# Norm, router and combining weights of a batch moved inside the attention of the next batch

## The reference

```python
mod = (_silu(L0_c) @ L0_wmod).reshape(L0_c.shape[0], 6, 1, -1)
h = _layernorm(x) * (1 + ca) + sa
x = x + ga * attention(h)             # scores * scale + relative-position bias, softmax, values, o_w
h = _layernorm(x) * (1 + cb) + sb
probs = sigmoid(h @ router_w.T + expert_bias)
top_w, top_idx = top_k(probs, 8);  top_w = 2.5 * top_w / (sum(top_w) + 1e-9)
h1w = silu(einsum('th,eih->eti', h, w_gate)) * combine.T[:, :, None]   # combine: top_w at top_idx, else 0
x = x + gb * (einsum('eti,ehi->th', h1w, w_down) + silu(h @ w_gate_shared.T) @ w_down_shared.T)
```

## Time and profile before

| | |
|---|---|
| median of 3 runs | 1000.38 us (1000.25 to 1002.1) |
| the profiled execution | 999.45 us, of which the span of instructions is 997.2 us |
| busy in the span | PE 946.7 us (95%), DVE 767.4 (77%), ACT 678.3 (68%), POOL 398.2 (40%) |
| chain that ended last, by engine | PE 84%, DMA 5%, DVE 4%, ACT 2%, POOL 2% |
| attention ends (last `attend`) | about 500 us from the span's start |
| mean granted clock of PE | 0.988 of full speed |

### The profile page before, as it was taken

One profiled execution on the slowest core, in us unless ns is written; L12 is line 12 of the kernel. 1 busy time (PEld: TensorE's weight loads), 2 busy tenths in 40 slices (PEclk: granted clock), 3 DMA queues, 4 the chain that ended last, 5 costly groups with the idle time before them and its releaser, 6 DMA issues.

```text
span 997.2 us, 15699 instructions
## 1 busy us (share of the span) xinstructions
PE 946.7 (95%) x4592; PEld 685.8 (69%) x4592; DVE 767.4 (77%) x1452; ACT 678.3 (68%) x1168; POOL 398.2 (40%) x260
## 2 busy tenths in 40 slices
PE   4889999999999999999979699999999999999997
PEld 2546666666666666666524578888888888888886
DVE  5757667766676666767546689999999999999997
ACT  4656666666666666666536577777777777777775
POOL 0668888888888888888800000000000000000000
PEclk9999999999999999999979899999999999999999
DMA  7985445445553564355002999999999999999991
GB/s 210 274 224 125 97 118 127 117 95 128 128 120 81 117 149 110 82 128 127 22 0 75 213 218 221 220 220 223 222 221 225 221 222 223 222 222 222 222 208 43
DMA packets 71105, 160.57 MB, mean 161 GB/s; under 512 B 10272, under 2 KB 36192, under 8 KB 60944
## 3 DMA queue, kind: packets, MB, share of 16 engines
q1 hardware_dynamic: 71056, 159.97, 71.2%
HBM read 105.60 MB, written 2.42 MB: 108 GB/s over the span
## 4 chain that ended last, share of the span: by engine, by line
PE 84%; DMA 5%; DVE 4%; ACT 2%; POOL 2%; SPq 1%; issue 1%; POOLq 0%; ACTq 0%; DVEq 0%
PE ps L620 40%; PE ps L433 11%; PE ps L420 10%; PE ps L409 5%; PE ps L411 5%; PE ps L383 4%; PE ps L446 2%; PE ps L394 2%; POOL prob L858 2%; DMA strips<-in_L_ffn_w_down 2%; DMA k_low<-qk 2%; DVE prob L975 1%; DMA strips<-comb_rows 1%; DMA comb_rows<-strips 1%; PE ps L538 1%
## 5 line engine op out<-in xcount | busy, mean ns | idle before, releaser
L858 POOL TENSOR_SCALAR prob<-prob,rinv 128x512 f32<-128x512 f32 x256 | 398.1, 1568 | 96.4 <-DVE rinv L992 94.3
L706 ACT ACTIVATE prob<-prob,nmax 128x512 f32<-128x512 f32 x256 | 182.9, 715 | 139.5 <-DVE nmax L975 139.5
L620 PE MATMUL ps<-hT,wT 128*128 128x512 f32 x960 | 243.9, 390 | 0.3 <-DVE wT L1144 0.3
L1163 DVE TENSOR_TENSOR PT<-v_sb,strips 128x1024 f32<-128x1024 f32 x160 | 195.9, 1224 | 43.1 <-ACT v_sb L830 29.3
L830 ACT ACTIVATE v_sb<-ps 128x1024 f32<-128x1024 f32 x160 | 164.4, 1028 | 65.2 <-PE ps L620 65.1
L620 PE MATMUL ps<-stack,wT 128*128 128x512 f32 x640 | 198.4, 392 | 9.5 <-DVE wT L1150 9.5
L620 PEld LDWEIGHTS ps<-hT,wT 128*128 128x128 f32 x960 | 180.5, 188 | 38.9 <-ACT strips L805 1.1
L1150 DVE TENSOR_TENSOR wT<-PT,stack 128x1024 fp32r<-128x1024 f32 x160 | 195.0, 1219 | 0.0
L204 DVE COPY PT<-ps 128x512 f32<-128x512 f32 x128 | 88.5, 691 | 137.9 <-PE ps L420 135.2
L822 ACT CAST stack<-PT 128x1024 fp32r<-128x1024 f32 x160 | 166.6, 1041 | 9.5 <-DVE PT L1163 9.5
L420 PEld LDWEIGHTS ps<-ident,prob 128*128 128x128 f32 x1024 | 114.4, 140 | 75.9 <-POOL prob L858 50.9
(11 more groups left out here) (105 smaller groups left out, 742.8 us busy)
## 6 DMA issues: line engine op xcount, KB each, us to landing
strips<-comb_rows SPq DMA_DIRECT2D x158, 512.0 KB, 12.3
stack<-qk SPq DMA_DIRECT2D x128, 256.0 KB, 3.9
k_low<-qk SPq DMA_DIRECT2D x64, 128.0 KB, 3.9
hT<-qk SPq DMA_DIRECT2D x64, 128.0 KB, 3.8
strips<-bias_rows SPq DMA_DIRECT2D x3, 1792.0 KB, 14.7
strips<-in_L_ffn_w_gate SPq DMA_DIRECT2D x80, 64.0 KB, 10.4
strips<-in_L_ffn_w_down SPq DMA_DIRECT2D x80, 64.0 KB, 12.3
strips<-bias_rows SPq DMA_DIRECT2D x2, 896.0 KB, 5.3
```

Source lines behind the costliest of these rows:

```text
L620: last = nc.tensor.matmul(ps[:, bank + c, :], weights(a), rows(m, c), start=start and k == 0, stop=stop and k == 2, skip_group_check=True)
L706: nc.scalar.activation(prob[:, u, :], prob[:, u, :], ACT.Exp, bias=nmax[:, u:u + 1], scale=-1.0, accum_out=rsum[:, u:u + 1]).then_inc(s_ex ...
L858: nc.gpsimd.tensor_scalar(prob[:, u, :], prob[:, u, :], rinv[:, u:u + 1], None, ALU.mult).then_inc(s_prob, 1)
L1163: nc.vector.tensor_tensor(weighted[:, k % 4, :], silu[:, k % 2, :], cb[:, r, half * HALF:(half + 1) * HALF], ALU.mult).then_inc(s_mul, 1)
```

## The change

What the transition did for all four batches is done for batch b - 1 inside pairs 2 to 7 of batch b, for b = 1, 2, 3 (`route` in the code):

- pair 2: aggregate of the statistics and + eps on DVE; POOL raises the variance to the power -0.5 (before: Sqrt on ACT, reciprocal on DVE)
- pair 3: `norm2` on DVE after the first two biases, its transposes on PE, `modulate2` on DVE, `h2_high` on ACT before `qk_high`
- pair 4: `logits` on PE before `attend`, both `sigmoids` on ACT after the first two exponentials, `h2_low` on DVE
- pairs 5 and 6: half of `transpose_sigmoids` each on PE before `attend`, and half of `keep_top` each on DVE after the fourth bias
- pair 7: both halves of `transpose_comb` on PE, their copies on ACT; the store is issued by SP in pair 9

The results go to the banks `BANK_PROJ`, so PE first waits in `bank_free`. The last batch is still routed after its attention, among the steps of the first expert round, which now runs all four expert pairs for tokens 0 to 1023 first and then for tokens 1024 to 2047 (`step_of_first`). Rows and weights for the first half are loaded during the last two pairs of attention. The low keys of odd pairs have a buffer of their own (before: part of `hT`), and the shared expert's gate runs in three passes with split weights.

```diff
-        k_low = sb("k_low", [P, 2, S], F32R)
-        kLow = (k_low[:, :, :], hT[:, 0, :, :])
+        kLow = sb("kLow", [P, 2, 2, S], F32R)
...
+        router_tmp = [router_first[:, :]] * (B - 1) + [work[:, 6144:7168]]
+        xn2 = [tmp[:, 0:S].rearrange("p (n d) -> p n d", d=D) for tmp in router_tmp]
+        h2 = [tmp[:, S:2 * S] for tmp in router_tmp]
+        comb = [tmp[:, 0:QT * E].rearrange("p (n e) -> p n e", e=E) for tmp in router_tmp]
+        probsT, probsT2 = router_rows[:, 0:S], router_rows[0:E - P, S:2 * S]
+        combT, combT2 = probsT, probsT2
...
+        def router_bank(n):
+            return BANK_PROJ + n % 2
+        ROUTER_A, ROUTER_B = 2, 3
+        def step_of_first(k):
+            return k % DEPTH, k // DEPTH
+        def step_of(k):
+            return divmod(k, 2)
...
+            def store_comb(b):
+                sp.wait_ge(s_cev, 2 * (b + 1))
+                sp.dma_start(flat[0:P, b * S:(b + 1) * S], combT).then_inc(s_cst, 16)
+                sp.dma_start(flat[P:E, b * S:(b + 1) * S], combT2).then_inc(s_cst, 16)
...
+            sp.wait_ge(s_ttr, (B - 1) * G + UNITS * 6)
             for r in range(DEPTH):
                 load_weights(0, r)
-            flat = comb_rows.rearrange("n two t -> (n two) t")
-            for b in range(B):
-                sp.wait_ge(s_cev, 2 * (b + 1))
-                sp.dma_start(flat[0:P, b * S:(b + 1) * S], combT[:, b * S:(b + 1) * S]).then_inc(s_cst, 16)
-                sp.dma_start(flat[P:E, b * S:(b + 1) * S], combT2[:, b * S:(b + 1) * S]).then_inc(s_cst, 16)
-                if b == 1:
-                    sp.wait_ge(s_cst, 64)
-                    load_rows(0, 0, slice(0, HALF), s_first_rows)
+            sp.wait_ge(s_cst, 64)
+            for r in range(DEPTH):
+                load_rows(0, r, slice(0, HALF), s_first_rows)
+            store_comb(B - 2)
+            store_comb(B - 1)
             sp.wait_ge(s_cst, 32 * B)
-            load_rows(0, 0, slice(HALF, T))
-            for r in range(1, DEPTH):
-                load_rows(0, r)
-            with sp.Fori(0, EPAIRS // DEPTH - 1) as i:
+            for r in range(DEPTH):
+                load_rows(0, r, slice(HALF, T))
+            for r in range(DEPTH):
+                sp.wait_ge(s_w, r + 1)
+                load_weights(1, r)
+            for r in range(DEPTH):
+                sp.wait_ge(s_mul, DEPTH + r + 1)
+                load_rows(1, r)
+            with sp.Fori(1, EPAIRS // DEPTH - 1) as i:
...
+            def bank_free(b, n):
+                last = b == B - 1
+                pe.wait_ge(s_qkl, b * HPAIRS + (min(n + 2, HPAIRS) if last else n + 2))
+                pe.wait_ge(s_vc, b * HPAIRS + (min(n + 1, HPAIRS) if last else n + 1))
...
+                if route is not None and n == 4:
+                    bank_free(b, n)
+                    logits(route, router_bank(n), 0)
+                    logits(route, router_bank(n + 1), 1)
+                if route is not None and n == 5:
+                    bank_free(b, n)
+                    transpose_sigmoids(route, router_bank(n), 0)
+                if route is not None and n == 6:
+                    bank_free(b, n)
+                    transpose_sigmoids(route, router_bank(n), 1)
+                if route is not None and n == 7:
+                    bank_free(b, n)
+                    transpose_comb(route, router_bank(n), 0)
...
+                if route is not None and n == 4:
+                    pe.wait_ge(s_sig, 2 * (route + 1))
...
+                if route is not None and n == 3:
+                    bank_free(b, n)
+                    transpose_normed(route, router_bank(n))
...
+                if route is not None and n == 7:
+                    pe.wait_ge(s_cev, 2 * route + 1)
+                    transpose_comb(route, router_bank(n), 1)
...
+                if route is not None and n == 3:
+                    pe.wait_ge(s_h2, route + 1)
+                if route is not None and n in (5, 6):
+                    pe.wait_ge(s_kept, 2 * route + n - 4)
+                if route is not None and n == 7:
+                    pe.wait_ge(s_cev, 2 * (route + 1))
...
+            late = B - 1
+            shared_down(0)
+            shared_down(1).then_inc(s_sd, 1)
+            first_gate(0)
+            transpose_normed(late, ROUTER_A)
+            first_gate(1)
+            logits(late, ROUTER_B, 0)
+            logits(late, ROUTER_A, 1)
+            first_gate(2)
+            first_gate(3)
+            first_down(0)
+            transpose_sigmoids(late, ROUTER_A, 0)
+            transpose_sigmoids(late, ROUTER_B, 1)
+            pe.wait_ge(s_h2l, B)
+            first_gate(4)
+            first_down(1)
+            first_gate(5)
+            first_down(2)
+            first_down(3)
+            pe.wait_ge(s_kept, 2 * B)
+            transpose_comb(late, ROUTER_A, 0)
+            transpose_comb(late, ROUTER_B, 1)
+            pe.wait_ge(s_cev, 2 * B)
+            shared_gate(2)
+            shared_gate(3)
+            shared_down(2)
+            shared_down(3).then_inc(s_sd, 1)
+            first_gate(6)
+            first_gate(7)
+            first_down(4)
...
+            def h2_high(b):
+                act.wait_ge(s_h2, b + 1)
+                nc.scalar.copy(hT[:, b, HIGH, :], h2[b]).then_inc(s_h2h, 1)
...
+            def sigmoids(b, banks):
+                for part, (rows, to) in enumerate(((slice(0, P), probsT), (slice(0, E - P), probsT2))):
+                    act.wait_ge(s_lg, 2 * b + part + 1)
+                    if b >= 1:
+                        act.wait_ge(s_cst, 32 * b)
+                    nc.scalar.activation(to, ps[rows, banks[part], :], ACT.Sigmoid,
+                                         bias=ebias[rows, part:part + 1]).then_inc(s_sig, 1)
...
+                if route is not None and n == 4:
+                    sigmoids(route, (router_bank(n), router_bank(n + 1)))
...
+                if route is not None and n == 3:
+                    h2_high(route)
...
+            def invert_deviation(b):
+                tiles = slice(QT * b, QT * (b + 1))
+                pool.wait_ge(s_var2, b + 1)
+                nc.gpsimd.tensor_tensor(rstd[:, tiles], mv[:, tiles, 1], minus_half[:, :], ALU.pow).then_inc(s_rstd2, 1)
...
+                        if b >= 1 and n == 2 and u == 4:
+                            invert_deviation(b - 1)
...
+            def norm2(b):
+                dve.wait_ge(s_rstd2, b + 1)
+                for t in range(QT):
+                    n = QT * b + t
+                    last = nc.vector.tensor_scalar(xn2[b][:, t, :], x_all[:, b, t * D:(t + 1) * D],
+                                                   mv[:, n, 0:1], rstd[:, n:n + 1], ALU.subtract, ALU.mult)
+                last.then_inc(s_xn2, 1)
...
+            def keep_top(b, bank, part):
...
+                dve.wait_ge(s_back, 2 * b + part + 1)
+                if part == 0:
+                    dve.wait_ge(s_lg, 2 * (b + 1))
+                    dve.wait_ge(s_h2l, b + 1)
+                for t in range(2):
+                    last = nc.vector.max(top8[:, first + t, :], probs[t])
+                then(last)
+                def replace(t):
+                    return nc.vector.match_replace(comb[b][:, first + t, :], top8[:, first + t, :], probs[t], 0.0)
+                nc.vector.tensor_reduce(sums, top8[:, first:first + 2, :], AX.X, ALU.add).then_inc(dve_step, 1)
+                replace(0)
+                dve.wait_ge(dve_step, steps[0] + 1)
+                nc.vector.tensor_scalar_add(sums, sums, SUM_EPS).then_inc(dve_step, 1)
+                replace(1)
+                dve.wait_ge(dve_step, steps[0] + 2)
...
+                nc.vector.tensor_tensor(kept, ps[:, bank, 0:2 * E], kept, ALU.subtract).then_inc(s_kept, 1)
+                dve.wait_ge(s_kept, 2 * b + part + 1)
+                for t in range(2):
+                    n = QT * b + first + t
+                    last = nc.vector.tensor_scalar(comb[b][:, first + t, :], comb[b][:, first + t, :],
+                                                   tsum[:, 1, n:n + 1], None, ALU.mult)
+                if part == 1:
+                    last.then_inc(s_comb, 1)
...
+                if route is not None and n == 3:
+                    norm2(route)
+                if route is not None and n == 4:
+                    h2_low(route)
...
+                if route is not None and n == 2:
+                    moments(route)
+                if route is not None and n in (5, 6):
+                    keep_top(route, router_bank(n), n - 5)
...
+            first_weigh(0)
+            modulate2(late, ROUTER_A)
+            first_weigh(1)
+            product_low(0, 0)
+            h2_low(late)
+            first_weigh(2)
+            product_low(0, 1)
+            first_weigh(3)
+            product_low(0, 2)
+            keep_top(late, ROUTER_A, 0)
+            keep_top(late, ROUTER_B, 1)
+            product_low(0, 3)
+            first_weigh(4)
+            first_weigh(5)
```

(6 more changed lines are left out.)

457 lines of the change are left out of this document (221 added, 236 removed).

## The result

| | before | after |
|---|---|---|
| median of the runs | 1001.24 us (4 runs, 1000.25 to 1002.87) | 1036.97 us (4 runs, 1034.76 to 1045.59) |
| profiled execution, span | 997.2 us | 1033.0 us |
| last copy of `oT` (end of attention) | 500.14 us | 553.90 us |
| from there to the end of the span | 497.1 us | 479.1 us |

The ratio is 1.037, 95% interval 1.031 to 1.043: slower by 3.7%. Forecast were 1020 us and 1000 to 1030. The direction held; the time lies outside. A few executions of any kernel here run long without a change of the kernel; the ratios and intervals of this document leave them out, the medians have them in.

The account below looks back on a forecast made before the run. Attention was taken as bound by PE's order of work, the expert stage as tied between PE and DMA rate; 999.45 + 39.6 (attention) - 20 (transition) = 1019.05 us profiled, so 1020 us, range 1000 to 1030.

Parts of the forecast that it names:

- Waits added to TensorE: In attention, TensorE's waits in bank_free lengthen pairs 4 to 7 by 14.7 us, from nothing to some 17.
- Attention: Attention grows by 39.6 us: 15.2 + 14.7 + 1.7 + 7.2 + 0.8.
- bank_free: Pairs 4 to 7: 11 waits of 1.18 us for qk_low, plus 1.7 from h2_high, together 14.7 us.
- keep_top: Pairs 5 and 6: half a keep_top takes 2.65 us on DVE, PE waits 1.2 us six times, 7.2 us.
- norm2: Pair 3 on DVE: 1.05 us inserted, 0.55 lost, three times, 1.7 us.
- TensorE's work and the small copies: In attention: PE's transposes and logits add 15.2 us; pair 7's copies and first-weight casts add 0.8.
- Table loads: Pair 4 on ACT: two loads of 1.28 us cost 0, since PE is late there itself.
- Rival (d): Pair 4: ACT's switches hold exponentials, attend waits about 2.7 us more in three pairs, 2.8 after attention: 1031; chance 0.04.
- Rival (b): In attention, waits are half as long, as DVE's chain is partly pulled forward while PE stands: 1008 us; chance 0.08.
- The transition: Between attention and steady expert steps: the ninth product comes at about 556 instead of 575.8, a gain of 20 us.
- Rival (a): In attention, waits and insertions vanish in slack, only PE's own added work counts: 995.6 us, faster; chance 0.14.
- Rival (c): In the transition, the store is pushed out or round 1's rows come 10 us late: 1030 us; chance 0.12.

Follow-up runs that it names:

- behind_attend: wait_moved with the router's block of pairs 4 to 7 put behind the two attends in TensorE's order; median 1013.67 us, ratio 1.010 to before.
- top_split: wait_moved with keep_top cut behind the reciprocal, the rest placed behind the fifth and sixth add_bias; median 1015.00 us, ratio 1.011 to before.
- before_wait: The kernel before with one line added, TensorE's wait for the five small loads ahead of pair 2 of the first batch; median 1013.53 us, ratio 1.010.
- both: The changed kernel with the edits of wait_moved, behind_attend and top_split together; median 1006.17 us, ratio 1.002 to before.
- rows_early: both, but the first expert round weights second-half tokens with first-half rows, loaded early (result differs in that round); median 999.21 us, ratio 0.996 to before.
- wait_moved: The changed kernel with TensorE's wait for the five small loads moved to before the second batch; median 1023.12 us, ratio 1.019 to before.
- token_major_2: token_major with the last two of four replacements as their own piece and the last two pieces moved to pair 6; median 998.77 us, ratio 0.996 to before.
- token_major: On top of wait_moved, logits with tokens on partitions, no sigmoid transposes, keep_top for four tiles in four pieces; median 999.92 us, ratio 0.998 to before.

## Why the prediction was wrong

**The step that failed is the list of added waits.** The part "Waits added to TensorE" names `bank_free` and nothing else. The change moves one more wait of TensorE, `pe.wait_ge(ld["small"], 80)`, from behind attention, where the loads had landed 400 us before, to pair 2 of the first batch. It appears in no term, no rival and no bound, and is worth 13.4 us: 1020 + 13.4 = 1033. The profile of before had what was needed: TensorE starts pair 2 at 61.01, and SyncE issues the last of the five loads, behind the stack of pair 3, at 69.98, with 3.2 us to landing (timeline of SyncE, and DMA issues from 55 to 75 us, of before):

```profile
69.98 0.43 SPq L291 DMA_DIRECT2D ebias<-in_L_ffn_expert_bias  x1
```

```profile
ebias<-in_L_ffn_expert_bias SPq DMA_DIRECT2D x1, 0.1 KB, 3.2
```

By these rows it is there at 73.2, and a wait for it at 61.01 costs about 12.2 us, an estimate close to the 13.4 measured.

**Attention otherwise**, forecast 39.6, is 40.9, point by point for three batches:
- `bank_free`: forecast 14.7. TensorE's waits on L1042 are 4.8 + 6.7 + 2.1 = 13.6 us, 11 of them, 1.05 to 1.59 each. By behind_attend, 10.4 of them come back when the router's work stands elsewhere.
- `keep_top`: forecast 7.2. It is six waits of 1.50, 9.0, since half a `keep_top` lasts 3.1 and not 2.65. One small scaling (L1159) takes 0.48 there, while GpSimd is at work on the probabilities, and 0.17 in the transition, where GpSimd stands; whether that is the reason was not tested. top_split returned 9.3.
- `norm2`: forecast 0.55 a batch, is 0.24.
- TensorE's work and the small copies: forecast 15.2 + 0.8. What is left of 40.9 is 17.6.
- Table loads: forecast 0, because TensorE is late there itself, and 0 they were. behind_attend took that lateness away, and 1.06 us a batch appeared. Rival (d) falls.

The terms are off by -1.1, +1.8, -1.0 and +1.6; that their sum is only 1.3 off is luck in part. Rival (b), the waits half as long, falls with them: the waits on `qk` and behind `keep_top` make 22.6 us where 21.9 were forecast.

**The transition**, forecast 20, gave 18.0 in this trace; since the rest scatters by some 4 us, that can't be told from the forecast. Product 8 stands 54.7 us after the last copy of `oT`; I had 55.9. Two stretches behind it are slower than carried over. The first is from the ninth to the thirteenth product: 12.5 us, not 10.8 (before has 11.3 there, the other kernels with the new transition 11.1 to 12.5). The windows of after (start:end, us, busy of TensorE, granted clock, DMA share, GB/s) for products 4 to 8, the first steps behind them and the steady stretch:

```profile
593.90:609.90 16.00, 8.76 (x22) 0.59 1.06 235
609.90:629.90 20.00, 20.00 (x88) 0.99 1.03 219
640.00:740.00 100.00, 100.00 (x443) 1.00 1.05 217
```

In the 16 us of products 4 to 8, while their rows come in, TensorE is busy for 8.76 us, its granted clock is mostly the lower level of 1.2 GHz (0.59 in the mean), and the matmuls beside these products run at it. The second is the last 147 steps: 399.8 us where before took 398.4. Seven of the kernels with the new transition have 399.8 and none has less; before_wait has 398.4. The loads run at 217 GB/s for 220, but both has 221 from 640 to 940 us at the same 399.8, so the rate is not shown as the cause, and it stays open. The power on GpSimd took 1.04 us, twice what I took and inside its bounds. That TensorE mostly waits from 500 to 560 us, as the prediction says of before, is a misreading without effect on the sum: it is busy for 43.35 of these 60 us, at a granted clock of 0.86.

**Rival (a)**, that waits vanish in slack, is refuted by behind_attend, top_split and both: of 22.6 us of waits on `qk` and behind `keep_top` they returned 19.4. **Rival (c)**, that the store or the rows of round 1 come 10 us late, falls too: product 8 stands 1.2 us ahead of the sum. The 6.3 us that rows_early gives back, where the last batch's rows are not waited for, were in the sum already.

The sum with the missing term: 999.45 + 13.4 + 40.9 - 18.0 = 1035.75 for the profiled execution, which took 1035.71. Two small things cancel in it: 0.6 us of the 40.9 is the shared gates, which lie behind the last copy of `oT` and so in the rest too, and what lies outside the span grew from 2.25 to 2.71 us.

## What to carry to other kernels

List every `wait` line of a diff with its old and its new place, and ask of each one when what it waits for is issued, before any instruction is priced: here a single line, which TensorE didn't need until a batch later, made more than a third of the loss. Where one engine is busy all the time, as TensorE is in this attention, a wait costs its full length; put the instruction behind independent work of the same engine, and cut a neighbour's long piece to the length of that neighbour's gaps. When a wait is taken away, look at what it hid: the table loads were free behind `bank_free`, and cost 1.4 us a batch without it.

## What was not expected of the hardware

- A load of 0.1 KB landed 2.0 us after its issue in a nearly empty queue, and 13.2 us after it behind 1792 KB of strips issued 5 us before it.
- The idle of TensorE for `k` at pair 2 of the first batch differed between kernels that are alike there: 4.02 us in wait_moved, 6.50 in token_major_2, with the first `project_out` from -0.4 to +3.0 us against before. The last 147 steps, the same code in all kernels with the new transition, took 399.8 us in seven of them, 400.7 in two, 403.1 and 404.7 in the others. So a difference of under 5 us between single executions says nothing here unless it is located in the stretch that the edit changes.
- In both the four attends at the end of attention took 3.65 us; in token_major_2 5.35, and in token_major 5.28. The granted clock is 1.00 in both from 519 to 524 us, and 0.74 in token_major_2 from 513 to 519.5. The 1.7 us took back a quarter of the 6.5 that token_major_2 had won against both up to there. Ahead of them lie the same two waits in each, 0.89 and 0.83 us:

```profile
519.87 3.65 PE L453 MATMUL ps<-PT,v_sb 128*64 128x512 f32 x16 [0.83 <-issue]
```

```profile
513.89 5.35 PE L454 MATMUL ps<-PT,v_sb 128*64 128x512 f32 x16 [0.83 <-issue]
```

Why the clock falls in the token_major kernels and not in both stays open.
